# A graph-attention layer and a two-of-four expert layer: last loads, last products and loop of the expert stage rearranged, three weight matrices loaded from ACT's queue

## The reference

```python
def layer(x, adj):
    n = layernorm(x)
    q, k, v = n @ Wq.T, n @ Wk.T, n @ Wv.T + bv          # 12 heads of 32
    a = einsum('bnhd,bmhd->bhnm', q, k) * 384**-0.5 + adj[:, None]
    a = softmax(where(all(a == 0, -1), -inf, a)); a = nan_to_num(a)
    x1 = x + (einsum('bhnm,bmhd->bnhd', a, v) @ Wo.T + bo)
    u = layernorm(x1)
    logits = u.mean(nodes) @ router_w.T + router_b        # 4 experts
    gates = softmax of the 2 greatest logits of each graph
    h = act_e(u @ w1[e] + b1[e])      # 768 wide; gelu, silu, mish, gelu
    y = sum over the 2 experts of gate * (h @ w2[e] + b2[e]) + u
    return x1 + layernorm(y) * ln_g + ln_b
```

## Time and profile before

| | |
|---|---|
| median of 3 runs | 1660.92 us (1660.24 to 1660.93) |
| the profiled execution | 1659.58 us |
| its span, first to last instruction | 1657.8 us |
| PE busy | 1598.8 us, 96% |
| DVE, ACT, POOL busy | 1179.8, 957.1, 827.4 us |
| mean granted clock of TensorE | 0.990 |
| DMA | 188.19 MB, 114 GB/s |
| chain that ended last, by engine | PE 87%, DVE 5%, issue 3%, ACT 3% |

### The profile page before, as it was taken

The page is one execution under the profiler, slowest core; times in us unless marked ns, Lnnn a source line. Parts: engine busy times, 40 slices in busy tenths (PEclk is TensorE's granted clock), DMA queues, the critical chain, the costliest instruction groups (busy, mean ns, idle before and its releaser), DMA issues.

```text
span 1657.8 us, 45212 instructions
## 1 busy us (share of the span) xinstructions
PE 1598.8 (96%) x12756; PEld 1533.7 (93%) x12757; DVE 1179.8 (71%) x3677; ACT 957.1 (58%) x2821; POOL 827.4 (50%) x1235
## 2 busy tenths in 40 slices
PE   8999999999999999859999999999999999999997
PEld 7999999999999999759999999999999999999997
DVE  5888888888888878737755665676677667566764
ACT  6899999999999988832422222333334323243431
POOL 4888888888888877612232333232323223322333
PEclk9999999999999999979999999999999999999999
DMA  6444443355555533872222222222221222222220
GB/s 194 144 141 140 133 141 128 136 173 171 179 178 172 175 127 124 293 292 63 63 73 72 71 72 72 72 72 72 72 72 57 64 71 70 72 72 72 72 69 33
DMA packets 93743, 188.19 MB, mean 114 GB/s; under 512 B 10336, under 2 KB 57440, under 8 KB 91872
## 3 DMA queue, kind: packets, MB, share of 16 engines
q1 hardware_dynamic: 91520, 169.39, 31.3%
q10 hardware_dynamic: 2016, 16.52, 2.7%
HBM read 108.80 MB, written 77.07 MB: 112 GB/s over the span
## 4 chain that ended last, share of the span: by engine, by line
PE 87%; DVE 5%; issue 3%; ACT 3%; POOL 1%; DMA 1%; DVEq 1%; ACTq 0%; POOLq 0%; SPq 0%
PE bank L423 67%; PE bank L497 5%; PE bank L622 4%; PE bank L450 3%; PE bank L520 3%; PE bank L537 2%; PE bank L529 1%; PE bank L506 1%; DVE half_t L1289 1%; DVE inverse L1296 1%; DVE inverse L1292 1%; ACT inverse L889 1%; ACT at_hi L856 1%; DMA ut_scratch<-ut_out 1%; DVE hid L1184 1%
## 5 line engine op out<-in xcount | busy, mean ns | idle before, releaser
L423 PE MATMUL bank<-w_hi,ut_in 128*128 x1536 | 423.8, 343 | 10.1 <-DVE hid L1184 8.9
L685 ACT ACTIVATE prob<-att,neg_max 128x128 f32<-128x128 f32 x768 | 297.3, 390 | 14.8 <-DVE neg_max L1044 11.2
L423 PEld LDWEIGHTS bank<-w_hi,ut_in 128*128 128x128 f32 x1536 | 281.5, 189 | 15.2 <-issue 15.0
L880 ACT ACTIVATE hid<-hid 128x384 f32<-128x384 f32 x192 | 95.1, 526 | 318.0 <-DVE hid L1184 305.2
L423 PE MATMUL bank<-w_hi,at_hi 128*128 x768 | 258.3, 336 | 5.0 <-DVE at_lo L1261 5.0
L1012 POOL TENSOR_SCALAR rs_z<-mv_z 128x1 f32<-128x1 f32 x64 | 14.7, 230 | 497.0 <-DVE mv_z L1315 450.0
L1261 DVE SCALAR_TENSOR_TENSOR at_lo<-bank,gate_col,at_hi 128x384 fp32r<-128x384 f32 x256 | 146.1, 612 | 162.9 <-ACT at_hi L856 162.9
L423 PE MATMUL bank<-w_lo,ut_in 128*128 x768 | 258.2, 336 | 0.0
L423 PE MATMUL bank<-w_hi,at_lo 128*128 x768 | 257.0, 335 | 0.0
L423 PE MATMUL bank<-w_lo,at_hi 128*128 x768 | 256.6, 334 | 0.0
L856 ACT ACTIVATE at_hi<-bank,gate_col 128x384 fp32r<-128x384 f32 x256 | 134.6, 577 | 170.0 <-PE bank L622 168.2
(11 more groups left out here) (135 smaller groups left out, 3826.5 us busy)
## 6 DMA issues: line engine op xcount, KB each, us to landing
xu_scratch<-xu SPq DMA_DIRECT2D x64, 384.0 KB, 2.3
ut_scratch<-ut_out SPq DMA_DIRECT2D x64, 384.0 KB, 2.7
ut_in<-ut_scratch SPq DMA_DIRECT2D x64, 384.0 KB, 3.0
xz<-xu_scratch SPq DMA_DIRECT2D x64, 384.0 KB, 3.1
x_in<-in_x SPq DMA_DIRECT2D x32, 384.0 KB, 4.9
xu<-in_x SPq DMA_DIRECT2D x32, 384.0 KB, 4.2
out_dram<-xz SPq DMA_DIRECT2D x64, 192.0 KB, 1.9
w_lo<-in_L_ffn_w SPq DMA_DIRECT2D x4, 1152.0 KB, 6.0
```

What stands on the lines that cost most here:

```text
L423: last = nc.tensor.matmul(acc, lhs[c][a], rhs[c][b], start=start and n == 0, stop=stop and n == len(terms) - 1)
L685: nc.scalar.activation(prob[g][:, hh, :], att[g][:, head, :], ACT.Exp, bias=neg_max[g][:, head:head + 1], scale=-1.0, accum_out=row_sum[g] ...
L880: nc.scalar.activation(hid[k][:, s], hid[k][:, s], ACT.Gelu).then_inc(a_ready[k], 1)
```

## The change

It has these parts. At the beginning the query, value and output matrices are loaded from ACT's queue, and only the key matrix from SP's. The router's product uses one constant matrix of 1/128 and weights multiplied into the pooled sums by DVE (`weigh`), 3 products in place of 12 for each half. Memory is laid out anew; w2_hi and w2_lo are one tile `w2_both`, loaded in eight column pieces of unequal size from step 61 on, and b1 in step 60; b2 is loaded by SP at the start of the second stage. In step 64 PE transposes all of the probabilities of graph 63 before `project_o(62)`; for graphs 62 and 63 DVE makes ot_hi and ot_lo itself. ACT takes all exponentials of graph 63 at once, applies the first activation inside step 66, and no longer waits for all stores ahead of the second stage. The banks of F are doubled (`hid_ps[k]`), so F waits for the job two before. The end of a graph has two fused operations on DVE and one on POOL (`x_based`, x1 plus ln_b). The output bias of both jobs is added in the second. The last job's transposes come right after those of the job ahead of it, with tiles of their own. The loop has 2 rounds over 28 graphs.

```diff
-    w2_dram = nc.dram_tensor("w2_scratch", (2, E, P, FC, D), F32, kind="Internal").ap()
+    w2_dram = nc.dram_tensor("w2_scratch", (P, 2, E, FC, D), F32, kind="Internal").ap()
...
-            with engine.Fori(1, B // 4 - 1) as i:
-                for m in range(4):
-                    step(i * 4 + m, m, i)
+            with engine.Fori(0, 2) as i:
+                for j in range(B // 2 - 4):
+                    step(i * (B // 2 - 4) + 4 + j, j % 4, i * (B // 8 - 1) + 1 + j // 4)
...
-        hid_ps, at_ps, y_ps = bank[0:2], bank[2:4], bank[4:6]
+        hid_ps, at_ps, y_ps = (bank[0:2], (bank[7], bank[6])), bank[2:4], bank[4:6]
...
+        def act_tiles(b, k):
+            if last_job(b, k):
+                return tuple(ut_in[i][:].rearrange("p s c n -> p (s c) n") for i in range(2)) + (hid_ps[0],)
+            return at_hi, at_lo, at_ps
...
             load_x(0)
-            load_projection(0)
             load_projection(1)
             load_x(1)
-            load_projection(2)
...
-            load_projection(3)
...
-                if h == B + 1:
-                    sp.wait_ge(xbo_done, B)
-                    sp.wait_ge(v_done, B)
+                if h == B:
+                    sp.wait_ge(o_mm, B - 2)
                     sp.wait_ge(ut_stored[1], 16)
                     load_ut(1, 1)
...
-                for e in range(E):
-                    for c in range(DC):
-                        last = nc.tensor.matmul(bank[7][:, D + e * ROUTED:D + (e + 1) * ROUTED], rw_wide[:, c, e, :], pooled[:, graphs, c],
+                for c in range(DC):
+                    last = nc.tensor.matmul(bank[7][:, D:D + E * ROUTED], ones[:], weighed[:, c].rearrange("p e b -> p (e b)"),
...
-                    reached(pe, hid_done, 2 * i + s - 1)
+                    reached(pe, hid_done, 2 * i + s - 3)
...
-                if has(h - 2):
+                if has(h - 2) and h != B:
                     project_o(h - 2)
                 if has(h - 1):
                     transpose_probs(h - 1, 0)
                     transpose_probs(h - 1, 1)
+                if h == B:
+                    transpose_probs(B - 1, 2)
+                    project_o(B - 2)
...
-                        transpose_act(b - 1, k)
+                        if not last_job(b - 1, k):
+                            transpose_act(b - 1, k)
+                        if last_job(b - 1, k + 1):
+                            transpose_act(b - 1, k + 1)
...
         def _(act):
+            for m in (0, 2, 3):
+                w = (Wq, Wk, Wv, Wo)[m]
+                act.dma_start(w_raw[m][:], w.rearrange("(c p) d -> p c d", p=P)).then_inc(w_loaded[m], 16)
...
-            act.wait_ge(routed, 1)
-            for g in range(2):
-                for p in range(2):
-                    act.wait_ge(xu_stored[p][g], 16 * (B // 4))
-                act.wait_ge(ut_stored[g], 16 * (B // 2))
...
+                    act.wait_ge(routed, 1)
+                    for g in range(2):
+                        act.wait_ge(xu_stored[0][g], 16 * (B // 4))
+                    activate(0, 0, choice(0, 0))
...
-                    reached(pool, zn_done, b - 1)
-                    nc.gpsimd.tensor_tensor(z, z, lng_wide[:], ALU.mult).then_inc(zg_done, 1)
-                    nc.gpsimd.tensor_tensor(z, z, x1, ALU.add).then_inc(zx_done, 1)
-                    nc.gpsimd.tensor_tensor(z, z, lnb_wide[:], ALU.add).then_inc(out_ready, 1)
+                if graph(b, -1):
+                    x1 = xz[(m - 1) % 4][:, 0, :]
+                    nc.gpsimd.tensor_tensor(x1, x1, lnb_wide[:], ALU.add).then_inc(x_based, 1)
...
+                if n >= B - 2:
+                    nc.vector.tensor_copy(flat(ot_hi[g][:]), flat(ot[g][:])).then_inc(ot_hi_done, 1)
+                    nc.vector.tensor_tensor(flat(ot_lo[g][:]), flat(ot[g][:]), flat(ot_hi[g][:]).bitcast(F32), ALU.subtract).then_inc(ot_lo_done, 1)
...
+                nc.vector.scalar_tensor_tensor(out=z, in0=z, scalar=mv_z[:, 0:1], in1=lng_wide[:], op0=ALU.subtract, op1=ALU.mult).then_inc(z_centred, 1)
...
-                nc.vector.tensor_scalar(z, z, mv_z[:, 0:1], rs_z[:], ALU.subtract, ALU.mult).then_inc(zn_done, 1)
+                nc.vector.scalar_tensor_tensor(out=z, in0=z, scalar=rs_z[:], in1=xz[m][:, 0, :], op0=ALU.mult, op1=ALU.add).then_inc(out_ready, 1)
```

More of the change, by code:

```diff
@@ L112, in gnn_moe_kernel @@
         pt = [sb(f"pt{c}", [P, BANK], F32, s1) for c in range(PTC)]
         inv_t = sb("inv_t", [P, DC, N], F32, s1)
-        inv_sum = [sb("inv_sum0", [P, HEADS, HEAD], F32, s1)]
+        inv_sum = [sb(f"inv_sum{g}", [P, HEADS, HEAD], F32, s1) for g in range(2)]
+        ot, ot_hi, ot_lo = [], [], []
+        for g in range(2):
+            ot.append(sb(f"ot{g}", [P, DC, N], F32, s1))
+            ot_hi.append(sb(f"ot_hi{g}", [P, DC, N], F32R, s1))
+            ot_lo.append(sb(f"ot_lo{g}", [P, DC, N], F32R, s1))
@@ L134, in gnn_moe_kernel @@
[L134 to L141 removed]
+        ones = sb("ones", [P, P], F32, s1)
@@ L407, in expert_step @@
                     load_rest()
+                if isinstance(b, int) and b == 2:
+                    sp.wait_ge(routed, 2)
+                    load_xz(3, 3)
                 if graph(b, -2):
@@ L849, in choice @@
                 return act.value_load(cell, min_val=0, max_val=E - 1)
-            def split_act_hi(b, k, m):
-                i = b * K + k
-                reached(act, at_mm, i + 1)
-                col = (m * K + k) % 4
-                for s in range(2):
-                    nc.scalar.activation(flat(at_hi[:, s * DC:(s + 1) * DC, :]), at_ps[s][:, 0:HALF],
-                                         ACT.Copy, scale=gate_col[:, col, 1:2]).then_inc(at_hi_done, 1)
             def activate(b, k, e):
@@ L885, in invert, with split_act_hi @@
+            def split_act_hi(b, k, m):
+                i = b * K + k
+                reached(act, at_mm, i + 1)
+                reached(act, gate_copied, i + 1)
+                col = (m * K + k) % 4
+                hi, _, banks = act_tiles(b, k)
+                for s in range(2):
+                    nc.scalar.activation(flat(hi[:, s * DC:(s + 1) * DC, :]), banks[s][:, 0:HALF],
+                                         ACT.Copy, scale=gate_col[:, col, 1:2]).then_inc(at_hi_done, 1)
             def invert(b, k, e):
@@ L919, in _ @@
             nc.gpsimd.memset(seed_out[:], SEED_D)
+            nc.gpsimd.memset(ones[:], 1.0 / N)
             for e in range(E):
```

372 lines of the change are left out of this document (215 added, 157 removed).

## The result

The changed kernel takes 1640.89 us (median of 4 runs, 1639.5 to 1641.74), the one before 1660.93 (4 runs): ratio 0.9879, 95% interval 0.9862 to 0.9896. It is faster, by 20.0 us in place of the 35 forecast, and lies outside the range of 1615 to 1637. The profiled execution took 1641.37 us (span 1639.2).

A forecast was written before the change was run, and what follows sets the result against it. PE's products were taken as the bound, with PE's idle time the main saving. 1659.58 + 0.4 - 2.1 - 22.0 - 6.0 + 0.5 - 5.3 = 1625.1 us, 1626 on the median's scale; range 1615 to 1637.

The forecast's parts named there:

- The beginning, +0.4: Start: three matrices on ACT's queue share the engines with the first x, which could delay it; 0.4 us slower.
- The router, -2.1: Router's product near 596 us: 24 passes become 6, the first half's saving counted in full; 2.1 us faster.
- Between the stages, -22.0: Transition between first and second stage: PE's waits for `ot_lo` and the first activation shrink; 22.0 us faster.
- in the change ACT's loads are spread: Transition, up to the last `attend`: residual load alone on the engines from 697, POOL not waiting; 6.2 us faster.
- the step of -11.9: Transition, T of job 0: ACT's wait for the last store of u transposed goes, last pooled sum remains; 11.9 us faster.
- The second stage, -5.5 with the loop: Second stage: doubled banks and a removed loop edge give -6.0 us, the long loop +0.5.
- The term of -3.0 for doubled banks: Second stage, after mish jobs with k = 1: F no longer waits, 0.5 us back six times; 3.0 us faster.
- The -4.4 for DVE's edge: Second stage: the one loop edge falling behind a mish job, which stalls DVE and PE, is gone; 4.4 us faster.
- covered by idle time: Second stage: DVE's added work, 0.75 us a graph, hidden by its idle time (busy 395 of 600 us); otherwise 48.
- The end, -5.3: End: last S follows at once (-2.3), one DVE operation replaces four operations after the last normalisation (-3.0); 5.3 us faster.
- The DMA engines are the bound: Rival, between the stages: w2 lands at about 735, first S moves little, transition gives -12: 1636 us; chance 0.17.
- Long code stalls the branches: Rival, second stage: branches leave fetched code on DVE and ACT, 4.0 us after each of 17 mish jobs: 1694; chance 0.04.

The follow-up runs named there:

- e7: Changed kernel, step-61 loads held for the residual behind `ot_hi`, last u before first activation, graph 2's biases behind `at_lo`, loop of four graphs: 1624.77 us.
- e8: e7 with the query, value and output matrices issued by the sync engine again: 1624.59 us.
- e2: Changed kernel with ACT's two loads of step 61 held until the residual of graphs 60 and 61 has landed: 1632.42 us.
- e9: e8 with a third tile for u transposed of graph 63, so ACT need not wait for the store of graph 61: 1622.7 us.
- e10: e9 with PE's wait ahead of each half of F as if there were one pair of banks: 1623.7 us.
- e13: Kernel before the change with 50 increments of an unused semaphore at the head of DVE's program: 1650.7 us, single run.
- e4: Changed kernel with the two output biases of graph 2 moved behind `at_lo` of job (2,0) on DVE: 1637.75 us.
- e3: Changed kernel with the old loop of 4 graphs (14 rounds) in the second stage: 1636.67 us.

## Why the prediction was right and wrong

- **The beginning, +0.4, measured +1.7 in the two profiles.** In time no difference can be measured (e7 and e8). The sign was right, and the size is inside the scatter of the runs: kernels that begin alike reach the router's product 1.6 us apart. By the Trainium skill (DMA: Bandwidth & Descriptors, "Issuing engines are not separate DMA queues") no more than the issue time was to be had, and e7 and e8 agree: 1624.77 and 1624.59.
- **The router, -2.1, measured -1.9.** Right.
- **Between the stages, -22.0, measured -8.7.** Here the prediction failed, at the step "in the change ACT's loads are spread ... the residual load has the engines for itself from 697". For graphs 62 and 63 it held: POOL did not wait for their residual at all. For 60 and 61 the load lay under the loads that the spread had moved ahead: last `attend` at 717.88 in place of 714.61, +3.3 where I had -6.2. e2 gives 8.5 us of the time back. A moved transfer has to be set against all that shares the engines at its new place; I did that only where a wait stood already.
- The second failure there is in the step of -11.9, "What is late next is the last sum for the pooled rows ... some 2 us after PE is free". The wait for the store of graph 63 is gone as forecast, but the copy ahead of that sum waited for the store of graph 61, which the prediction did not name. From the last `attend` to T of job 0 the change gained 10.9 us (25.0 to 14.1) where 1.4 + 11.9 = 13.3 were forecast, and from there to T of job 2 1.2 where 3.7 - 1.2 = 2.5 were. With the 9.5 us at `attend` these make up the 13 us missed. T of job 0 came 7.7 us sooner than before, at 731.99; e9, without the wait for the store, takes 1.9 us less than e8.
- **The second stage, -5.5 with the loop, measured -5.0.** The sum was right by luck. The term of -3.0 for doubled banks is nothing (e10). The -4.4 for DVE's edge are real (that block went from 11.80 to 7.10), but due to the place of the old body in the code: e13 gains 7.9 us in this stage without any change of the work, 3.9 of them in that block. With both bodies well placed the changed code in the short loop (870.3, and 868.6 in e9, where the biases are moved too) is within 3 us of the old (871.1), and the long loop of the change adds 3.7 (874.0), of which PE's one edge is 2.6 (2.4 of waiting), and the lower clock in the block at 764 another 1.6; half a us elsewhere goes the other way. The edge of PE itself was bounded at 4.8 and priced at 0.5, since I took PE to be ahead of its fetch.
- The added DVE work "covered by idle time" was not, in one block: about 2.2 us, and 3.8 with the lower clock behind the wait (e4). It is the error of taking a mean over the whole stage.
- **The end, -5.3, measured -4.7.** Right, step by step.
- **The rivals.** "The DMA engines are the bound" had the nearest time (1636), and w2 was whole at 736 as it said, but by another mechanism: S waited for w2 only once the stalls ahead were gone (e9). "Long code stalls the branches" did not come, at one edge in place of 17 stalls.

## What to carry to other kernels

When bulk loads are moved earlier, list every small load of the other queues at the new place, and who waits for it; one 384 KB load beside 2.6 MB cost 8.5 us here. Hold the bulk behind it, but behind the engine's own due work too. And before a loop is changed for the sake of its edge, shift its code by some dozens of instructions and look at the instruction queue's packets: that alone moved this kernel's second stage from 889.4 to 871.1 us, and a comparison of two versions can contain it.

## What the runs showed that was not expected

- The place of a loop body in DVE's code is worth up to 18 us of some 880 (889.4 against 871.1), with packets of instructions going from 8 to 73 as the sign of it in a loop of four graphs. A longer body can be the one that fits (e3).
- Two hardware queues shared the DMA engines by packets and not by bytes (365 against 327 packets in 9 us, 0.68 against 2.75 MB), and in the 4 us before that unevenly: 14 packets of the sync engine's passed beside 167 of ACT's. The residual's packets have 1536 bytes, those of ACT's two loads 9216 and 11776, so turns by packets leave it the smaller share.
- The first 600 us of kernels that begin alike differ by up to 1.6 us, and part of it comes from the first products: 18 transposes of weights took 2.8 us in e4 and 4.0 in the changed kernel, with a granted clock of 1.00 in the windows of both, so that the traces do not say why.
